# Indirect DMAs with a bound: the index of an unfilled expert slot beyond the table

## What is computed

```python
    def _L0_ffn_ref(x, router_w, w1, b1, w2, b2):
...
        logits = jnp.einsum('tc,ec->te', x_flat, router_w)
        probs = jax.nn.softmax(logits, axis=-1)
        top_w, top_idx = jax.lax.top_k(probs, K)
        top_w = top_w / (jnp.sum(top_w, axis=-1, keepdims=True) + 1e-09)
        h = jnp.einsum('tc,efc->tef', x_flat, w1) + b1[None]
        h = jax.nn.relu(h)
        y = jnp.einsum('tef,ecf->tec', h, w2) + b2[None]
        sel = jnp.take_along_axis(y, top_idx[:, :, None], axis=1)
        out = jnp.einsum('tkc,tk->tc', sel, top_w)
...
    def _L1_ffn_ref(x, router_w, router_bias, bank_mag, bank_freq, bank_phase, bank_down, norm_w):
...
        scores = jnp.einsum('btd,nd->btn', x, router_w) + router_bias
        topv, topi = jax.lax.top_k(scores, TOPK)
        weights = jax.nn.softmax(topv, axis=-1)
        fx = x.reshape(b * t, d)
        mag = jnp.einsum('td,ndh->tnh', fx, bank_mag)
        freq = jnp.einsum('td,ndh->tnh', fx, bank_freq)
        hidden = jnp.tanh(mag) * jnp.cos(jax.nn.softplus(freq) + 0.1 + bank_phase[None, :, :])
        out_all = jnp.einsum('tnh,nhd->tnd', hidden, bank_down)
...
        out = jnp.einsum('tkd,tk->td', sel, weights.reshape(b * t, TOPK)).reshape(b, t, d)
        out = out * jax.lax.rsqrt(jnp.mean(out * out, axis=-1, keepdims=True) + EPS) * norm_w
```

## Time and profile before

| what | value |
| --- | --- |
| time, median of 3 runs | 834.06 us (833.79 to 834.38) |
| profiled execution: its time, its span | 836.8 us, 835.0 us |
| PE, DVE, POOL, ACT busy | 66%, 62%, 52%, 39% of the span |
| layer 0 experts, first gather to last scatter | 375.7 to 513.4 us |
| layer 1 experts: first gather, first and last scatter | 626.0, 732.3, 804.0 us |
| indirect DMAs | 88 gathers, 88 scatters |
| software DMA queue (all indirect DMAs) | 5632 packets, 11.55 MB |

### The profile page before, as it was taken

How to read it: one execution, slowest core, us unless ns; L and a number is a source line. 1 busy time by engine, 2 the same in 40 slices (tenths; PEclk the granted TensorE clock), 3 DMA queues, 4 the chain that set the end, 5 groups by cost and what they waited for, 6 DMA issues and landing times.

```text
span 835.0 us, 8658 instructions
## 1 busy us (share of the span) xinstructions
PE 555.1 (66%) x1876; PEld 291.8 (35%) x1877; DVE 521.8 (62%) x977; ACT 327.0 (39%) x629; POOL 433.0 (52%) x337
## 2 busy tenths in 40 slices
PE   3668889779878969527878785466415867376730
PEld 2313234333323323324656564234312322155520
DVE  5864698689597979393323233454492888766635
ACT  3365453464535623001222226565202655680003
POOL 0067878569767967116556542212516754065633
PEclk9869789798978978857989898579556899789865
DMA  4054345223222320281111123000102114211132
GB/s 156 0 148 158 129 134 185 76 79 108 95 63 91 126 76 26 86 345 44 36 41 38 38 35 102 22 0 14 38 0 48 41 35 28 101 38 44 41 116 63
DMA packets 36658, 63.52 MB, mean 76 GB/s; under 512 B 5202, under 2 KB 22164, under 8 KB 36116
## 3 DMA queue, kind: packets, MB, share of 16 engines
q1 hardware_dynamic: 30996, 51.64, 18.6%
q0 software_dynamic: 5632, 11.55, 5.8%
HBM read 53.99 MB, written 9.18 MB: 76 GB/s over the span
## 4 chain that ended last, share of the span: by engine, by line
PE 43%; DVE 24%; issue 10%; ACT 8%; another core or an unknown queue 4%; DMA 4%; DVEq 3%; POOL 2%; SPq 1%; POOLq 0%; ACTq 0%
PE ps L937 12%; PE ps L1037 8%; DVE hs L1438 4%; PE ps L1022 4%; PE ps L906 4%; PE ps L931 3%; PE ps L1029 2%; DVEq L1503 2%; DVE prod L1448 2%; DVE h_tok L1241 2%; DVE p_hot L1329 2%; PE ps L1191 1%; PE ps L1106 1%; ACT h_tok L705 1%
## 5 line engine op out<-in xcount | busy, mean ns | idle before, releaser
L445 POOL TENSOR_TENSOR bu<-uT,b_sb 128x1024 f32<-128x1024 f32 x64 | 149.0, 2348 | 34.3 <-DVE uT L1418 34.3
L937 PE MATMUL ps<-prod,cst 128*128 128x512 f32 x256 | 142.9, 709 | 0.6 <-DVE yT L1458 0.6
L411 POOL DMA_INDIRECT y_dram<-ys,rows_i x88 | 85.5, 971 | 104.7 <-DVE ys L1671 47.2
L405 POOL DMA_INDIRECT xl<-h_dram,rows_i x88 | 88.3, 1003 | 49.8 <-issue 25.2
L456 POOL TENSOR_TENSOR prod<-hs,c_sb 128x1024 f32<-128x1024 f32 x32 | 75.1, 2348 | 59.9 <-DVE hs L1438 52.4
L602 ACT ACTIVATE ps<-dtT,neg_a 128x512 f32<-128x512 f32 x128 | 85.1, 683 | 51.6 <-DVE hs L1438 50.0
L1438 DVE TENSOR_TENSOR_SCAN hs<-ps,bu 128x512 f32<-128x512 f32 x64 | 74.0, 1207 | 27.2 <-ACT ps L602 24.4
L937 PEld LDWEIGHTS ps<-prod,cst 128*128 128x128 f32 x256 | 55.3, 227 | 92.4 <-issue 88.9
L1438 DVE TENSOR_TENSOR_SCAN hs<-ps,carry,bu 128x512 f32<-128x512 f32 x64 | 78.1, 1267 | 6.5 <-ACT ps L602 6.3
L931 PE MATMUL ps<-bc_f,sel_f 32*128 32x512 f32 x64 | 45.8, 803 | 50.0 <-DVE prod L1448 50.0
L1172 PE MATMUL ps<-mf_s,xt 128*128 x96 | 59.3, 706 | 22.6 <-ACT xt L671 13.6
(11 more groups left out here) (238 smaller groups left out, 960.7 us busy)
## 6 DMA issues: line engine op xcount, KB each, us to landing
b_sb<-b_rows SPq DMA_DIRECT2D x32, 512.0 KB, 4.5
c_sb<-b_rows SPq DMA_DIRECT2D x32, 256.0 KB, 3.6
w_s<-in_w SPq DMA_DIRECT2D x17, 256.0 KB, 4.0
mf_s<-in_mf SPq DMA_DIRECT2D x1, 4096.0 KB, 18.3
h_dram<-h_tok SPq DMA_DIRECT2D x8, 256.0 KB
b_s<-in_b SPq DMA_DIRECT2D x1, 2048.0 KB, 9.1
phase_s<-in_phase SPq DMA_DIRECT2D x1, 2048.0 KB, 22.6
down_s<-in_down SPq DMA_DIRECT2D x1, 2048.0 KB, 8.1
```

Source lines behind the costliest of these rows:

```text
L405: pool.indirect_dma_start(xl[:, j % XR, :], None, h_dram[l], bass.IndirectOffsetOnAxis(ap=rows_i[:, 0, j:j + 1], axis=0)).then_inc(loaded[ ...
L411: pool.indirect_dma_start(y_dram[l], bass.IndirectOffsetOnAxis(ap=rows_i[:, 1, j:j + 1], axis=0), ys[:, j % XR, :], None).then_inc(saved[j ...
L445: nc.gpsimd.tensor_tensor(bu[:, g % RING, :, :], uT[:, c % 2, :, :], b_sb[:, k % BRING, g % 2, :].unsqueeze(1).broadcast_to([P, ND, CHUNK] ...
L937: last = nc.tensor.matmul(bank(Y_BANK + d), ident, prod[:, g % RING, d, :], start=n == 0, stop=n == NS - 1)
```

## The change

- `rows_i` gets the index of unfilled slots in another way. With NOROW = 65536, a picked value of 0 becomes 65536, so that the scatter's index is 65535 and the gather's 65536 - T = 63488; for filled slots both are as before.
- Both indirect DMAs get `bounds_check` (T for the gather, 2T - 1 for the scatter) and `oob_is_err=False`: a row whose index lies beyond is left out, the gather leaves what was in the buffer, the scatter writes nothing.
- `y_dram` has 2T rows in both layers, and `spare` is gone with its two DVE operations. `h_dram` keeps its T + 1 rows, and the row of zeros at its head is still stored (L338 to L340); only no slot reads it any more.
- In the built program POOL gets 176 instructions more: one register move ahead of each indirect DMA, which loads the bound. The wait that stood on the DMA (`rows_ready`, `xt_ps` or `dn_sb`) stands on that move.

```diff
@@ -44,6 +44,7 @@
 RMS_EPS2 = 1e-6
 BIG = 64.0
 LOWEST = -3.0e38
+NOROW = 65536.0
 MAGIC = 1.5 * 2.0 ** 23
 TURN = 6.283185
 PI = 3.141592653589793
@@ -80,8 +81,7 @@
 def adaln_two_layers(nc, x, consts, vecs, w_in, conv_rows, w_x, w_dt, w_out, w1, b1, w2, b2, wmod,
                      w4, wo, mf, phase, down, norm_w, rbias1, out):
     h_dram = [nc.dram_tensor(f"h_dram{l}", (T + 1, C), F32, kind="Internal").ap() for l in range(2)]
-    y_dram = [nc.dram_tensor(f"y_dram{l}", (2 * T + n * P, C), F32, kind="Internal").ap()
-              for l, n in enumerate((ST0, ST1))]
+    y_dram = [nc.dram_tensor(f"y_dram{l}", (2 * T, C), F32, kind="Internal").ap() for l in range(2)]
     b_rows = nc.dram_tensor("b_rows", (NCHUNK, 2 * NS, CHUNK), F32, kind="Internal").ap()
     x_rows = x.rearrange("(t p) c -> p t c", p=P)
     out_rows = out.rearrange("(t p) c -> p t c", p=P)
@@ -234,7 +234,6 @@
         row_of, e = place("row_of", [P, 2, NTILE], at=e)
         p_iota, e = place("p_iota", [P, P], at=e)
         p_next, e = place("p_next", [P, 1], at=e)
-        spare, e = place("spare", [P, ST1], at=e)
         picked, e = place("picked", [P, ST1], at=e)
         rows_f, e = place("rows_f", [P, 2, ST1], at=e)
         w4_s, e = place("w4_s", [P, 4, C], at=e)
@@ -403,13 +402,14 @@
                 if j >= XR:
                     pool.wait_ge(S[f"xt_ps{l}"], j - XR + 3)
                 pool.indirect_dma_start(xl[:, j % XR, :], None, h_dram[l],
-                                        bass.IndirectOffsetOnAxis(ap=rows_i[:, 0, j:j + 1], axis=0)).then_inc(loaded[j % XR], 16)
+                                        bass.IndirectOffsetOnAxis(ap=rows_i[:, 0, j:j + 1], axis=0),
+                                        bounds_check=T, oob_is_err=False).then_inc(loaded[j % XR], 16)
 
             def put_rows(l, j, ys):
 
                 pool.wait_ge(S[f"dn_sb{l}"], j + 3)
                 pool.indirect_dma_start(y_dram[l], bass.IndirectOffsetOnAxis(ap=rows_i[:, 1, j:j + 1], axis=0),
-                                        ys[:, j % XR, :], None).then_inc(saved[j % XR], 16)
+                                        ys[:, j % XR, :], None, bounds_check=2 * T - 1, oob_is_err=False).then_inc(saved[j % XR], 16)
 
             def weigh_tiles(l, st):
 
@@ -1299,8 +1299,6 @@
                                                in1=cst[:, K["eiota"]].unsqueeze(1).broadcast_to([P, P // E1, E1]), op0=ALU.mult, op1=ALU.add)
                 then(nc.vector.tensor_reduce(p_next[:, :], cst[:, K["tri"]], axis=AX, op=ALU.add))
                 then(nc.vector.tensor_scalar(p_next[:, :], p_next[:, :], -1.0, float(P), ALU.mult, ALU.add))
-                then(nc.vector.tensor_scalar(spare[:, :], cst[:, K["jiota"]], float(P), float(2 * T), ALU.mult, ALU.add))
-                then(nc.vector.tensor_scalar(spare[:, :], spare[:, :], p_next[:, 0:1], None, ALU.add))
                 dve.wait_ge(S["rank_ps"], l + 1)
                 then(nc.vector.tensor_copy(route[:, 4, 0:n], ps[:, 2, 0:n]))
 
@@ -1340,12 +1338,11 @@
                 then(nc.vector.tensor_copy(picked[:, 0:st], ps[:, 3, st:2 * st]))
                 then(nc.vector.scalar_tensor_tensor(out=picked[:, 0:st], in0=ps[:, 3, 0:st], scalar=float(P), in1=picked[:, 0:st],
                                                     op0=ALU.mult, op1=ALU.add))
-                nc.vector.tensor_scalar(rows_f[:, 0, 0:st], picked[:, 0:st], T + 0.5, -float(T), ALU.is_ge, ALU.mult)
-                then(nc.vector.scalar_tensor_tensor(out=rows_f[:, 1, 0:st], in0=picked[:, 0:st], scalar=0.0, in1=spare[:, 0:st],
-                                                    op0=ALU.is_equal, op1=ALU.mult))
-                nc.vector.tensor_tensor(rows_f[:, 0, 0:st], rows_f[:, 0, 0:st], picked[:, 0:st], ALU.add)
-                then(nc.vector.scalar_tensor_tensor(out=rows_f[:, 1, 0:st], in0=picked[:, 0:st], scalar=-1.0, in1=rows_f[:, 1, 0:st],
-                                                    op0=ALU.add, op1=ALU.add))
+                then(nc.vector.tensor_scalar(rows_f[:, 1, 0:st], picked[:, 0:st], 0.0, NOROW, ALU.is_equal, ALU.mult))
+                then(nc.vector.tensor_tensor(picked[:, 0:st], picked[:, 0:st], rows_f[:, 1, 0:st], ALU.add))
+                nc.vector.tensor_scalar(rows_f[:, 1, 0:st], picked[:, 0:st], -1.0, None, ALU.add)
+                then(nc.vector.tensor_scalar(rows_f[:, 0, 0:st], picked[:, 0:st], T + 0.5, -float(T), ALU.is_ge, ALU.mult))
+                then(nc.vector.tensor_tensor(rows_f[:, 0, 0:st], rows_f[:, 0, 0:st], picked[:, 0:st], ALU.add))
                 nc.vector.tensor_copy(rows_i[:, :, 0:st], rows_f[:, :, 0:st]).then_inc(S["rows_ready"], 1)
                 dve.wait_ge(S["tiles_ready"], l + 1)
                 dve.wait_ge(S["pick_exp_done"], l + 1)
```

## The result

| | before | changed |
| --- | --- | --- |
| median of 20 runs | 833.81 us | 839.88 us |
| profiled execution: time, span | 836.8, 835.0 us | 838.68, 836.8 us |

The ratio of the times is 1.0072, with a 95% interval of 1.0047 to 1.0098. The change costs about 6 us where 3.8 us were forecast (833.81 is the median of more runs of before than the 834.06 that the prediction started from). Eight of the twenty runs of the changed kernel had a mean granted clock of 0.797 to 0.801 and took 840.15 to 847.59 us, while the median of the other twelve, at 0.809 to 0.818, is 838.46 us, so a part of the 6 us goes with the clock.

What follows compares the result with a forecast made beforehand. The prediction took the length of POOL's bursts of indirect DMAs to be on the path. Terms of +4.0 - 1.0 + 0.7 + 0.1 = +3.8 us on 834.06 gave 837.9 us, range 823 to 855.

Steps and rivals of the forecast that it cites:

- g = 0.04: POOL: what one indirect DMA adds to the pitch, from the register move ahead of it, 0.04 us; +4.0 us in all.
- rival 1: POOL: the move hides under the DMA before it and the comparison is free; 831.4 to 833.9 us, chance 0.27.
- one more dispatch between wait and DMA, 0.05 x 2 = +0.1: First gather of each layer: the added move delays its start by 0.05 us, +0.1 us for both layers.
- 30 g: Layer 1's down stage: 30 of the 48 scatters' added pitches were taken to count, between 0 and 48.
- 55 g: Layer 0's expert stage: added pitches of the opening gathers, seven further bursts and the tail together, 2.2 us.
- 5 g each: Layer 0: each of the seven chain pieces on an unknown queue should grow by about five added DMA pitches.
- 42 g: Layer 0's seven further bursts: six added pitches each lie between DVE's release and the stall's end.
- the sign named ahead: Layer 0: if the unknown-queue pieces change without a change of the burst, the reading of the bursts is wrong.
- the factor 100: Both expert stages: 100 us of time per 1 us added to POOL's pitch by each DMA, between 70 and 118.
- 15 g: Layer 1's up stage: the opening burst of fifteen gathers counts in full, the other 33 gathers are hidden.
- Ahead of the ranks: DVE before the ranks are read: without the spare-row operations the copy starts 0.50 us earlier per layer, -1.0 us.
- Behind the table: DVE between the picks and the cast: five operations in place of four, +0.36 us a layer, +0.7 us.

Runs made afterwards that it cites:

- Kept registers: The changed kernel with both bounds put into registers once at POOL's start: 831.44 us, ratio to before 0.9954 (loud chip); 781.58 us, 1.0010 (quiet chip).
- the bound alone: The kernel before with bounds above every index on both indirect DMAs: 842.51 us, ratio 1.0072 (loud chip); 783.50 us, 1.0040 (quiet chip).
- BATCHED = 1: The kernel before with layer 0's gathers and scatters alternating one by one, not in fours: 822.99 us, ratio 0.9830 (loud chip); 780.29 us, 0.9997 (quiet chip).

## Why the prediction came out as it did

The forecast was 837.9 us and slower by 0.46%; measured were 839.88 us and 0.72%, so direction and size are right. The total came near in part by luck: the largest term was of another kind than the one I priced, it did not show where I counted it (layer 0), and what made up for it was not in the sum: a start 0.50 us late at the long waits, and in eight of the twenty runs a lower granted clock.

- **The bare price of the move (g = 0.04).** The gap between two DMAs stayed 0.30 us: the move is hidden whenever POOL does not wait, as rival 1 had it. This agrees with the Trainium skill, page "Perfetto Trace Analysis", section "DMA Instruction — SWDGE (GPSIMD)", by which the sequencer goes on while the DMA ahead writes its descriptors. g came instead from the duration, 0.055 us for a gather and 0.017 for a scatter, where I took 0 for the check. The mean of the two, 0.036, is near 0.04 by luck. By the prediction's own counts it makes 12 x 0.055 + 7 x (4 x 0.055 + 2 x 0.017) + 15 x 0.055 = 3.3 us, and 30 x 0.017 = 0.5 for the down stage.
- **The wait on the move.** The step that failed is "one more dispatch between wait and DMA, 0.05 x 2 = +0.1". It was counted at the two first gathers alone and at 0.05 us each. It is 0.50 to 0.62 us a time: 1.12 - 0.50 = 0.62 and 1.02 - 0.50 = 0.52 at the two first gathers, 1.1 us together, and 0.50 at each scatter that waits for DVE. I had named it as what speaks against rival 1 and then priced it as one move. Kept registers bring the start back from 1.07 to 0.57 us on both kinds of chip, so it is the move's. My reading is that a DMA that carries its own wait has been made ready when the wait ends, and one behind a waiting move is made ready only then; the runs show the 0.50 us, not what fills it.
- **Layer 1's down stage.** 30 g = 1.2 us were forecast, 3.3 us and 3.2 us came. The place was right (its long waits are followed by a scatter that waited) and the cause is the 0.50 us, since kept registers with the same longer DMAs have 72.9 us. I had taken idle time of POOL there for something that hides a growth; on the loud chips it hid nothing of a later start, and on the quiet ones all of it.
- **Layer 0.** 55 g = 2.2 us were forecast; the stage grew by 0.4 and 0.9 us in two traces of the changed kernel and by 3.8 in one of the bound alone. The pieces on an unknown queue did not grow by 5 g each: there are six of 1.2 to 5.6 us where before had seven of 4.3 to 5.6, and in three of the seven bursts two scatters follow the gathers in place of one. The factor 42 g stood on a regular pattern that a small change shifts. By the sign named ahead (the pieces change in another way than the burst), the factor 100 is not borne out, and on a quiet chip the layer grew by 0.8 us. The stalls' length with BATCHED = 1 speaks for a part of the burst in it; it is not the whole of it, and on two other chips the stalls are absent. No number of this stage is settled.
- **Layer 1's up stage.** 15 g = 0.6 us forecast, with 4.4 us in one trace of the changed kernel, 0.4 in the other and 0.3 with the bound alone. The 4.4 go with a granted clock of 0.79 in place of 0.84, and BATCHED = 1, which has layer 1 as before, took 3.5 us more at 0.80. The two other traces fit the forecast, but differences of 0.4 us are too small to tell from one execution each.
- **DVE.** Ahead of the ranks: the copy starts 0.19 us after the operation before it, where it was 0.69 (358.24 to 358.93), a gain of 0.50 as forecast; 0.44 in layer 1. Behind the table: 367.74 to 369.20 is 1.46 us, before 1.14, so +0.32, and +0.32 in layer 1 (forecast +0.36 each). Right.
- **Landing.** The last scatter of layer 1 has 2.12 us in the chain in place of 2.24, though it writes nothing. The 0 was right to 0.1 us.
- **Leaving rows out.** The bound alone is above the changed kernel on the loud chip (842.5 and 838.1 us) and, against before, on quiet ones (1.0040 and 1.0016). So the rest of the change, less traffic and other index code, may give back some 2 to 4 us, of which DVE's net -0.3 us is the only part seen. Against it: the intervals overlap, the two executions on the loud chip differ in large part ahead of the first gather and in layer 0, and with all rows left out the one run on a quiet chip gained nothing. This stays open.

## What to carry to other kernels

In this program an operand that had to be put into a register ahead of an instruction took the wait with it. So look in the built program at which instruction carries the wait, count the places where the engine really waits, and price each with the start after release, not with the length of the move. Where a value is constant, put it into a register once: on the loud chip that kernel was 6.7 us faster, about half of it shown to be the move's, and on the quiet one no slower. Leaving rows out of an indirect DMA saved bytes and no time on POOL: with 0.10 MB moved in place of 8.42 a gather still took 1.000 us. Before a difference of some us is given to a change, set the stages of two executions side by side with their granted clock; here stages that the change didn't touch differed by 3 to 4 us with it.

## What the runs showed of the hardware that was not expected

- An indirect DMA with a bound takes POOL 0.997 to 1.000 us (gather of 128 rows of 512 bytes) or 0.982 to 0.985 us (scatter) in place of 0.945 and 0.967, whether none, some or all of its rows are left out; the packets stay 32 a DMA (5632 in all).
- A wait on a register move ahead of an indirect DMA makes it start 1.07 us after the start of the 0.29 us DVE operation that ends the wait; a wait on the DMA itself 0.57 us, also when the DMA reads its bound from a register.
- The same program takes 780.6 us on two chips and 834 to 835 us on others, with a mean granted clock of 0.836 and 0.81. In the two expert parts the loud ones have stalls of up to 5.6 us after rows of DMAs on POOL; layer 0's part takes 137.7 us there and 105.3 without. The change costs 0.72% and 0.43% on loud chips and 0.16%, within the error, on a quiet one.
- On loud chips the changed kernel's stage without indirect DMAs took 112.5 us at a mean granted clock of 0.66 in one execution and 116.1 at 0.62 in another, with the same 202 matmuls busy for 48.39 and 53.24 us.
